# Decoder on one core: part of the delta layer's sums moved from TensorE to VectorE, half of each normalization moved to GpSimd, and new order tables

## The reference

```
x = x + attn(layernorm(x)); x = x + xattn(layernorm(x), ctx); x = x + ffn(layernorm(x))   # layers 0 to 3
layernorm(x) = (x - mean(x)) / sqrt(var(x) + 1e-5)
```

```
attn = where(strict_lower, -(kb @ k.T), 0);  T = inv(I - attn)
o = einsum('blhp,blhpd->blhd', probs, paths)        # 5 paths
o = o * rsqrt(mean(o*o) + 1e-5) * norm_w;  out = o @ Wo
```

## Time and profile before

| | |
|---|---|
| median of 3 runs | 1532.43 us (1527.53 to 1540.35) |
| the profiled execution | 1539.65 us, its span 1537.8 us |
| mean granted TensorE clock | 0.964 |
| busy share: PE, PEld, DVE, ACT, POOL | 94%, 82%, 69%, 41%, 8% |
| fills in the queue of TensorE | 469 in part A, 361 in part C |

### The profile page before, as it was taken

One profiled execution on the slowest core, in us unless ns is written; L12 is line 12 of the kernel. 1 busy time (PEld: TensorE's weight loads), 2 busy tenths in 40 slices (PEclk: granted clock), 3 DMA queues, 4 the chain that ended last, 5 costly groups with the idle time before them and its releaser, 6 DMA issues.

```text
span 1537.8 us, 44388 instructions
## 1 busy us (share of the span) xinstructions
PE 1438.5 (94%) x19676; PEld 1264.5 (82%) x19676; DVE 1053.7 (69%) x2951; ACT 624.2 (41%) x1253; POOL 127.7 (8%) x267
## 2 busy tenths in 40 slices
PE   4999999999998689999989999999999999999996
PEld 3888888888884359989878989988998988998986
DVE  5758668577576948756777766577865667866666
ACT  4344353353355844532433533333542332552322
POOL 2111111111110000010000000000010010000000
PEclk8999999999999789999999999799998999999999
DMA  7000000000001110000000000000000000000000
GB/s 292 2 2 2 2 2 2 2 3 1 2 3 35 35 71 2 1 2 4 1 1 1 1 2 3 2 2 2 1 1 3 3 2 2 1 1 3 3 2 28
DMA packets 6526, 20.40 MB, mean 13 GB/s; under 512 B 2240, under 2 KB 4288, under 8 KB 5696
## 3 DMA queue, kind: packets, MB, share of 16 engines
q1 hardware_dynamic: 6336, 17.58, 3.2%
HBM read 16.53 MB, written 1.05 MB: 11 GB/s over the span
## 4 chain that ended last, share of the span: by engine, by line
PE 48%; DVE 10%; ACT 2%; issue 1%; POOL 1%; DVEq 0%; ACTq 0%
PE PS L2056 6%; PE PS L1917 6%; PE PS L1663 4%; PE PS L1629 4%; PE PS L1674 3%; PE PS L1642 3%; PE PS L1927 3%; PE PS L493 3%; DVE X L2434 2%; PE PS L1654 2%; PE PS L641 1%; PE PS L2366 1%; PE PS L2023 1%; DVE mx L591 1%; PE PS L502 1%
## 5 line engine op out<-in xcount | busy, mean ns | idle before, releaser
L493 PE MATMUL PS<-CC 128*128 128x128 f32 x1660 | 232.1, 283 | 0.0
L493 PEld LDWEIGHTS PS<-CC 128*128 128x128 f32 x1660 | 211.0, 197 | 4.9 <-issue 0.3
L482 POOL TENSOR_SCALAR SC<-mv 128x2 f32<-128x2 f32 x96 | 18.9, 197 | 1241.8 <-DVE mv L470 1241.4
L2056 PE MATMUL PS<-AR,PA 64*64 64x256 f32 (+43 forms) x2624 | 112.7, 301 | 0.8 <-issue 0.7
L1917 PEld LDWEIGHTS PS<-AR 64*64 64x64 f32 x3072 | 107.7, 140 | 6.6 <-issue 3.4
L1917 PE MATMUL PS<-AR 64*64 64x32 f32 (+1 forms) x3072 | 111.9, 223 | 1.0 <-issue 0.8
L641 PEld LDWEIGHTS PS<-vo,AR 128*64 128x64 f32 x2560 | 81.9, 138 | 16.5 <-issue 6.4
L474 DVE TENSOR_SCALAR xn<-X,mv,SC 128x128 f32<-128x128 f32 x192 | 57.7, 343 | 54.6 <-POOL SC L485 54.0
L2056 PEld LDWEIGHTS PS<-AR,PA 64*64 64x64 f32 x2624 | 88.7, 134 | 6.9 <-issue 3.2
L641 PE MATMUL PS<-vo,AR 128*64 128x18 f32 x2560 | 88.6, 212 | 4.7 <-DVE AR L1584 2.5
L591 DVE TENSOR_REDUCE mx<-PS 128x8 f32<-128x512 f32 x96 | 60.4, 681 | 18.7 <-PE PS L745 18.7
(11 more groups left out here) (419 smaller groups left out, 3102.0 us busy)
## 6 DMA issues: line engine op xcount, KB each, us to landing
WC<-in_cw SPq DMA_DIRECT2D x1, 5438.5 KB, 19.1
PA<-in_fd SPq DMA_DIRECT2D x1, 2624.0 KB, 9.8
PA<-in_stat SPq DMA_DIRECT2D x2, 1280.0 KB, 5.9
CC<-in_const SPq DMA_DIRECT2D x1, 1065.0 KB, 8.1
out<-X SPq DMA_DIRECT2D x1, 1024.0 KB, 5.1
PA<-in_aw SPq DMA_DIRECT2D x1, 975.0 KB, 11.5
AR<-in_raw SPq DMA_DIRECT2D x1, 832.0 KB, 8.1
AR<-in_intw SPq DMA_DIRECT2D x1, 576.0 KB, 9.1
```

Of the source, the lines that this page charges most:

```text
L493: T.matmul(bank[int(b)][:, 0:P], lhsT=ident, rhs=CC[:, 0:P], start=True, stop=True)
L2056: m = T.matmul(out_[:, :, first:SEQ], lhsT=FD[rows, tap:tap + 64], rhs=d.vp[rows, :, first + 1 - shift:SEQ + 1 - shift], start=starts, sto ...
```

## The change

Four edits:

1. Step 0 of the inversion: the mask is now the lower one (`low1`), and VectorE adds the two halves of the masked matrix and scales the sum. The 16 products `up0` are gone, 8 times (4 iterations, 2 streams).
2. The mix: the ten products `mixed` are gone, 8 times. VectorE sums the five paths with one `tensor_reduce` per tile; `mixed` lies in the arena, no longer in PSUM.
3. The norm: VectorE makes `xn` of tile 0 only, GpSimd that of tile 1, behind its own power. TensorE waits for each before its transpose. What GpSimd adds for the residual (`xb`) waits for VectorE's `xn0` instead of `xn1`, and stands behind GpSimd's new instruction.
4. All tables are new. Fills: 390 in part A (79 fewer), 362 in part C (one more); counted from one iteration's first L2a product to the next's, part C has 90, 90, 91 and 89 where it had 86, 86, 98 and 90.

```diff
@@ -47 +47 @@
     i64, j64 = i % 64, np.arange(64)[None, :]
-    for m in (1, 2, 4, 8, 16):
+    for m in (2, 4, 8, 16):
         c[f"up{m}"] = (i64 // (2 * m) == j64 // (2 * m)) & ((j64 // m) % 2 == 1) & ((i64 // m) % 2 == 0)
+    c["low1"] = (i64 // 2 == j64 // 2) & (i64 % 2 == 1) & (j64 % 2 == 0)
     c["across"] = (i64 < 32) & (j64 >= 32)
@@ -470 +471 @@
             V.wait_ge(*st.pool.at(f"{k}.rstd"))
-            for j in range(TS):
-                V.tensor_scalar(st.xn[:, j, :], st.x[:, j, :], st.mv[:, j, 0:1], st.sc[:, 2 + j:3 + j], ALU.subtract,
-                                ALU.mult).then_inc(*v.up(f"{k}.xn{j}"))
+            V.tensor_scalar(st.xn[:, 0, :], st.x[:, 0, :], st.mv[:, 0, 0:1], st.sc[:, 2:3], ALU.subtract,
+                            ALU.mult).then_inc(*v.up(f"{k}.xn0"))
             yield
@@ -485 +485 @@
             yield
+            G.wait_ge(*g.at(f"{k}.rstd"))
+            G.tensor_scalar(st.xn[:, 1, :], st.x[:, 1, :], st.mv[:, 1, 0:1], st.sc[:, 3:4], ALU.subtract,
+                            ALU.mult).then_inc(*g.up(f"{k}.xn1"))
+            yield
             yield
@@ -497 +501 @@
             yield
-            T.wait_ge(*st.dve.at(f"{k}.xn1"))
-            for j in range(TS):
-                m = T.transpose(st.ps[:, 0, j * P:(j + 1) * P], st.xn[:, j, :], ident)
+            T.wait_ge(*st.dve.at(f"{k}.xn0"))
+            T.transpose(st.ps[:, 0, 0:P], st.xn[:, 0, :], ident)
+            T.wait_ge(*st.pool.at(f"{k}.xn1"))
+            m = T.transpose(st.ps[:, 0, P:2 * P], st.xn[:, 1, :], ident)
             m.then_inc(*st.pe.up(f"{k}.xt"))
@@ -862 +867 @@
             yield from pool_norm(st, k)
-            G.wait_ge(*st.dve.at(f"{k}.xn1"))
+            G.wait_ge(*st.dve.at(f"{k}.xn0"))
             G.tensor_tensor(st.xb[:, :, :], st.x[:, :, :], bc(w(f"{k}_bo"), 1, TS), ALU.add).then_inc(
@@ -1107 +1112 @@
-        FILL_A = ("033333333333333333333333333333333333333333333300000000022111115511111000000000000115555111111111"
...
+        FILL_A = ("001133333333333333333333333333333333333222200331111551111000000000155111111115511101100000001111"
...
         TURNS_A = {
...
         }
@@ -1894 +1897 @@
                 self.pr, self.p4 = ar[:, 3072:4352], ar[:, 1536:2816].rearrange("p (n d) -> p n d", d=32)
-                self.mixed = ps[:, 0, 0:ST]
+                self.mixed = ar[:, 5632:5888]
                 self.sT, self.hg = ar[0:80, 4352:4352 + ST], ar[:, 4608:5120]
@@ -1960 +1963 @@
             yield
-            T.wait_ge(*v.at(f"{k}.pairs"))
-            products(f"{k}.up0", 2, d.up[0], lambda rows, n: cc("ident32")[rows, :])
-            yield
             for n in range(1, 5):
@@ -2014 +2014 @@
             m.then_inc(*p.up(f"{k}.logits"))
-            yield
-            for j in range(TS):
-                yield
-                T.wait_ge(*v.at(f"{k}.parts{j}"))
-                for c in range(5):
-                    o = 640 * j + P * c
-                    m = T.matmul(d.mixed[:, j * P:(j + 1) * P], lhsT=ident, rhs=d.pr[:, o:o + P], start=(c == 0),
-                                 stop=(c == 4))
-            m.then_inc(*p.up(f"{k}.mixed"))
             yield
@@ -2165 +2156 @@
             yield
-            A.wait_ge(*p.at(f"{k}.mixed"))
+            A.wait_ge(*v.at(f"{k}.mixed"))
             A.square(d.sq2, d.mixed).then_inc(*a.up(f"{k}.mixed_squares"))
@@ -2206 +2197 @@
             yield
-            mask(0, "up1", "pairs")
+            mask(0, "low1")
             yield
@@ -2216 +2207 @@
             yield
-            V.wait_ge(*p.at(f"{k}.up0"))
-            V.tensor_tensor(d.pc, d.bank[2], dd8, ALU.mult).then_inc(*v.up())
+            V.wait_ge(*v.now())
+            V.tensor_tensor(d.pc, d.up[0][:, :, 0:32], d.up[0][:, :, 32:64], ALU.add).then_inc(*v.up())
+            yield
+            V.wait_ge(*v.now())
+            V.tensor_tensor(d.pc, d.pc, dd8, ALU.mult).then_inc(*v.up())
             yield
@@ -2318 +2312 @@
                                 bc(lg[:, j, :].rearrange("p (h c) -> p c h", c=5), 3, 32),
-                                ALU.mult).then_inc(*v.up(f"{k}.parts{j}"))
+                                ALU.mult).then_inc(*v.up())
+            yield
+            V.wait_ge(*v.now())
+            for j in range(TS):
+                V.tensor_reduce(d.mixed[:, j * P:(j + 1) * P], d.pr[:, 640 * j:640 * j + 640].rearrange(
+                    "p (c n) -> p n c", c=5), AX, ALU.add).then_inc(*v.up(f"{k}.mixed" if j else None))
             yield
@@ -2559 +2558 @@
-        FILL_C = ("022222221100000000000211133333000000000003300000000000000111100000003311115514111111122222220011"
...
+        FILL_C = ("002222110000000001113333300000000000330000000000000000000000000000000000331115514111101111002222"
...
         TURNS_C = {
...
         }
                                     ("vector", vector_part_c, vector_aside_c), ("pool", pool_part_c, None)):
```

More of the change, by code:

```diff
@@ L1108, in pool_part_a @@
                 yield from pool_norm(st, "L1f")
-        FILL_A = ("033333333333333333333333333333333333333333333300000000022111115511111000000000000115555111111111"
-            "155110111110000000001111111111111111111133333333333333333333322222222222200000000444441500000000"
-            "000001155551111111111551101111100000000011111111111111111111333333333333333333333222222222222000"
-            "000004444415000000000000011555511111111115511011111000000000111111111111111111113333333333333333"
-            "3333322222222222200000000444441500000000000001155551111111111551101111000000000000000")
-        TURNS_A = {
-            "tensor": (21, 12, 20, 11, 10, 242, 21, 62, 20, 152, 11, 22, 21, 10, 11, 30, 11, 22, 11, 52, 11, 10, 22,
[17 rows of a table removed]
-            "scalar": (21, 20, 11, 10, 21, 20, 31, 10, 11, 20, 11, 20, 71, 30, 11, 40, 31, 10, 11, 40, 51, 30, 31, 20,
[6 rows of a table removed]
-            "vector": (21, 20, 11, 10, 11, 10, 61, 20, 11, 20, 11, 10, 11, 10, 11, 10, 11, 10, 11, 10, 11, 10, 11, 10,
[12 rows of a table removed]
-            "pool": (31, 30, 71, 70, 31, 30, 81, 80, 51, 50, 71, 70, 71, 70, 31, 30, 81, 80, 51, 50, 71, 70, 71, 70,
-                31, 30, 81, 80, 51, 50, 71, 70, 71, 70, 31, 30, 81, 80, 51, 50, 31, 30,),
+        FILL_A = ("001133333333333333333333333333333333333222200331111551111000000000155111111115511101100000001111"
+            "111111111111133333333333333333333222222222000000004444415000000000005511111115511100110000000111"
+            "111111111111113333333333333333333322222222220000004444415000000000005511111115511100110000000111"
+            "111111111111111333333333333333333322222222200000000444441500000000000155111111155111001100000000"
+            "000000")
+        TURNS_A = {
+            "tensor": (21, 22, 11, 20, 22, 10, 162, 21, 192, 20, 11, 12, 31, 32, 10, 11, 20, 11, 10, 22, 11, 10, 22,
[16 rows of a table added]
+            "scalar": (31, 30, 31, 20, 31, 10, 11, 40, 71, 30, 11, 40, 31, 10, 11, 40, 51, 30, 31, 20, 41, 30, 11, 20,
[6 rows of a table added]
+            "vector": (21, 20, 11, 10, 11, 10, 121, 20, 11, 20, 11, 10, 11, 10, 11, 10, 11, 10, 11, 50, 11, 10, 11,
[11 rows of a table added]
+            "pool": (41, 40, 81, 80, 41, 40, 91, 90, 61, 60, 91, 90, 81, 80, 41, 40, 91, 90, 61, 60, 91, 90, 81, 80,
+                41, 40, 91, 90, 61, 60, 91, 90, 81, 80, 41, 40, 91, 90, 61, 60, 41, 40,),
         }
@@ L2560, in pool_part_c @@
                 yield from pool_l3_ffn(st)
[L2562 to L2565 removed]
+        FILL_C = ("002222110000000001113333300000000000330000000000000000000000000000000000331115514111101111002222"
+            "110000000001113333300000000000330000000000000000000000000000000000331115514111101111002222110000"
+            "000002111333330000000000033000000000000000000000000000000000033111551411110111100222221100000000"
+            "01113333300000000000330000000000000000000000000000000000331115514111101111")
         TURNS_C = {
[L2567 removed]
[33 rows of a table removed]
[L2601 removed]
[15 rows of a table removed]
[L2617 removed]
[33 rows of a table removed]
[L2651 to L2652 removed]
+            "tensor": (21, 24, 11, 20, 11, 20, 24, 11, 24, 10, 51, 50, 21, 24, 21, 20, 24, 20, 54, 31, 24, 21, 30, 11,
[32 rows of a table added]
+            "scalar": (10, 21, 10, 31, 30, 11, 10, 31, 30, 21, 20, 13, 21, 13, 12, 10, 12, 13, 21, 10, 12, 13, 11, 12,
[15 rows of a table added]
+            "vector": (20, 21, 10, 21, 10, 21, 10, 11, 20, 51, 40, 21, 10, 21, 40, 81, 70, 11, 20, 31, 10, 33, 20, 21,
[31 rows of a table added]
+            "pool": (41, 40, 61, 60, 131, 130, 71, 70, 41, 40, 61, 60, 61, 60, 131, 130, 71, 70, 41, 40, 61, 60, 61,
+                60, 131, 130, 71, 70, 41, 40, 61, 60, 61, 60, 131, 130, 71, 70, 41, 40,),
         }
```

8 lines of the change are left out of this document (removed), and 227 rows, old and new, of tables (TURNS_A, TURNS_C).

## The result

The changed kernel takes 1541.72 us (median of 20 runs, 1535.28 to 1544.77) against 1535.67 us for the kernel before (20 runs): ratio 1.0036, 95% interval 1.0022 to 1.0050. It is a little slower, less than 1%. The forecast was 1496 us, the range 1472 to 1524 us: **the prediction was wrong**. Its profiled execution has a span of 1541.1 us at a mean granted clock of 0.964, the same as before, so the two traces can be set side by side.

A forecast was written before the change was run, and what follows sets the result against it. Prediction: the chain through the engines sets part A, TensorE bounds part C. From the median of 1532 us: -25 (part C) -15 (part A) +4 (clock) = -36, giving 1496 us; range 1472 to 1524 us.

The forecast's parts named there:

- GpSimd's half: Norm, part A: GpSimd's xn instruction taken as 0.41 us, transposes start 0.19 us sooner; with VectorE's relief, 15 us less.
- VectorE's relief of 0.26 us: Norm: VectorE has 0.26 us less ahead of the other stream's work, 48 times, 12.5 us if all on a chain.
- The fills say nearly the same: Part A: 79 fewer fills at 0.23 us each, 18.2 us, read as agreeing with the norm's at most 17 us.
- Products out, the mix: Part C: the ten products mixed leave TensorE, 2.23 us for each stream, 8 times: 17.8 us less.
- has 4 us more, hidden: Part C: VectorE's sums and reductions, less saved norm halves, add 4 us in some 970, hidden at 70% busy.
- Products out, step 0: Part C, inversion: the 16 products up0 leave TensorE, 0.95 us each time, 8 times: 7.6 us less.
- TensorE's queue equals the time in part C: Part C is TensorE's, so its queue being 25 us shorter, fills counted, makes the part 25 us shorter.
- The clock: Part C: long rounds of small products in every iteration may lower TensorE's granted clock: 4 us added.
- The norm gives nothing: Rival, part A: GpSimd waits for VectorE's half, missing fills become idle time: 1513 us, chance 0.20.
- GpSimd's half comes late: Rival, all 96 norms: GpSimd's half held up by contention, 0.63 us later: 1573 us, at half of them 1543; chance 0.07.
- The rule that I cited: Norm: VectorE and GpSimd contend for the shared SBUF port, making part A's gain a small loss; left out of the sum.

The follow-up runs named there:

- experiment 3: The changed kernel with VectorE again making xn of both tiles, no half on GpSimd: 1533.01 us, ratio 0.9992 to the kernel before.
- experiment 7: The changed kernel with xn made by VectorE alone and the mix summed by three additions instead of two reductions: 1529.08 us, ratio 0.9955.
- experiments 18: The kernel before, old order, with step 0 on VectorE and the mix's products replaced by one copy of one path (result incomplete): 1531.70 us, ratio 0.9975.
- experiment 13: The kernel before, on the old order, with only step 0 of the inversion moved to VectorE (products up0 gone): 1529.03 us, ratio 0.9970.
- experiment 6: The changed kernel with the removed products put back in the chains as unread ballast, 25 us of TensorE's time in part C: 1566.81 us, ratio 1.0200.
- experiment 14: The changed kernel with xn made by VectorE alone and one copy of one path in place of the mix's sum: 1529.78 us, ratio 0.9965.
- experiment 15: The changed kernel with stream 1's norm ahead of stream 0's last weighted additions at part C's three iteration joins: 1542.53 us, ratio 1.0058.
- experiment 11: The kernel before, on the old order, with only the mix summed by VectorE's reductions instead of TensorE's products: 1551.05 us, ratio 1.0111.

## Why the prediction was wrong

Of the 42 us between forecast and measurement 22 us are the norm's (7 us lost by experiment 3, where 15 us were to be won), some 6 us the sum's price (experiment 7), and the other 14 us are missing in part C otherwise: TensorE's products left and did not give their time.

- **GpSimd's half** (term -15 us). The step that failed is its price: 0.86 us, beyond both bounds (0.20 to 0.70 us). The upper bound was a row of another operation on twice the columns, the lower one an instruction with two constants on 2 columns. In the norm shown the second transpose comes 0.39 us later, with a half of median length some 0.34 us (an estimate: 0.05 us less), not 0.19 us sooner, and part A's iteration grows by 1.1 us. Edit 3 costs 12 us on the old order and 7 us on the new. Whatever VectorE's relief of 0.26 us gave elsewhere is in these numbers, and it did not make up for that.
- **"The fills say nearly the same"**. 79 fills fewer were read as gaps shorter by 18 us. Experiment 4 takes as many out of the old order, and part A's iterations stay at 107.1 us. I had named the test myself (idle time in place of a fill) and still let it support the 15 us.
- **Products out, the mix** (-17.8 us). Removed they are, and VectorE "has 4 us more, hidden" is the step that failed. It has 17.6 us more. The reductions make 6.4 us of the difference (19.4 us where I took 13.0 us); the rest I did not follow. On the old order it is not hidden: edit 2 alone costs 17 us. A busy share of 70% said nothing of the place: there the other stream's maxima stand behind the reductions, and TensorE waits for them. The term failed too, and not only its price: with a sum of 0.29 us the products' removal still gives nothing on the old order (experiments 18 and 13).
- **Products out, step 0** (-7.6 us). Right: 7.8 us off part C in the profile of experiment 13, 5 us by the ratio.
- **"TensorE's queue equals the time in part C"**. Half right: products in a chain cost their full time (experiment 6), but taking them out gives it only where nothing else is late next. On the new order, with the norm on VectorE and the cheaper sum, 7 us were gained (experiment 7) where the prediction had 25 us less 4 us of clock.
- **The clock** (+4 us). The long rounds of small products did not bring it down: 0.964 in both profiles, the iterations at 0.96 to 0.97. Nor were such rounds new: the kernel before has one of 93 records, some 48 products, in its first iteration too. The clock fell where I did not look, behind TensorE's long waits: on the old order those of 5 us and more, on the new one those of the joins.

```profile
1054.10:1058.10 4.00, 3.88 (x14) 2.79 (x14) 0.68 (x2) 0.37 (x1) 2.32 (x4) 0.50 0.01 2
```

- **The rivals.** "The norm gives nothing" had the right sign for part A and too small a size. "GpSimd's half comes late" named the right place, but expected contention. The rows speak for the instruction's own time. In the first pair below VectorE runs nothing more beside GpSimd's instruction, once its own half is done; in the second VectorE's half starts only after GpSimd's has ended, and other work of VectorE runs beside it:

```profile
87.73 0.35 DVE L474 TENSOR_SCALAR xn<-X,mv,SC 128x128 f32<-128x128 f32 x1 [1.11 <-POOL SC L485]
87.80 0.86 POOL L489 TENSOR_SCALAR xn<-X,mv,SC 128x128 f32<-128x128 f32 x1
```
```profile
928.20 0.80 POOL L489 TENSOR_SCALAR xn<-X,mv,SC 128x128 f32<-128x128 f32 x1
929.14 0.34 DVE L474 TENSOR_SCALAR xn<-X,mv,SC 128x128 f32<-128x128 f32 x1
```

  All 96 lie between 0.80 and 0.91 us, so the differences in what VectorE does beside it are worth 0.11 us at most; no row has VectorE idle all the time. The rule that I cited, of the Trainium skill ("SBUF — State Buffer", Who interferes with whom), foretold a small loss, and the sign agrees; as the mechanism of this loss it is not borne out. VectorE's half takes 346 ns in the median beside GpSimd's and took 342 ns before; three of the 96, which start 0.07 us behind GpSimd's (one at 788.89), take 0.45 us, where the longest before took 349 ns.

**What stays open.** By part C's rows TensorE idles 22.6 us more after than before. Its named waits say where: 15.5 us more for VectorE's `xn`, of which the joins make 11.5 us, 5.5 us for GpSimd's half and 2.8 us more for VectorE's gated products. They come with the new tables: TensorE idles 59.8 us in experiment 14, without GpSimd's half and nearly without the sum, and 60.1 us in experiment 6, with unread products where the old ones stood. What they cost is open: experiment 15 took 5.4 us off the waits for `xn` and gained nothing, and no run has the new tables alone.

## What to carry to other kernels

Before work is moved from the busiest engine to another, look in the trace at what that other engine does at that very place and who waits for it; its mean busy share does not tell. A count of filler products alone did not measure a gap here; the iteration's time and TensorE's idle time in it did. A price without a row of the same operation, size and access pattern needs bounds that are wide on the high side; two such prices were too low here, by factors of 2.1 and 1.5.

## What the runs showed of the hardware that I had not expected

- GpSimd's `TENSOR_SCALAR` with two column operands takes 0.65 us for 128x64 and 0.86 us for 128x128: 3.3 ns a column between the two, which leaves some 0.43 us (an estimate from these two sizes). VectorE takes 0.34 us for the same 128x128.
- VectorE's reduction of 128x640 to 128x128, with the reduced index outermost in memory, takes 1.25 us, more than 1024 columns reduced along memory (1.22 us). Three plain additions do the same for two tiles in 1.5 us instead of 2.5 us.
- The time of one kernel follows the clock from run to run. A line through 29 runs of the kernel before, with mean clocks of 0.960 to 0.972, gives 15.8 us less for each 0.01 more, about as if every us of TensorE at half level were half a us of the kernel; one through the 20 runs of the changed kernel, 0.962 to 0.971, gives 9.0 us.
- After its wait of 5.05 us in experiment 11 TensorE goes on at the half level from 1010.4 to about 1014.2, after that of 5.15 us in the changed kernel from 1054.1 to about 1058.2.
